# Gradient stage: silu outputs transposed by DMA as 16-bit planes, second layer moved to the end of a pair

## The reference, cut to what matters

```python
def _mlp(w1, b1, w2, b2, x):
    return jax.nn.silu(x @ w1.T + b1) @ w2.T + b2
...
k_flat = x_in.reshape(-1, D)
v_flat = out_swa.reshape(-1, D)
def loss_fn(params):
    pred = _mlp(*params, k_flat)
    return 0.5 * jnp.sum((pred - v_flat) ** 2)
grads = jax.grad(loss_fn)((w1, b1, w2, b2))
upd = jax.tree_util.tree_map(lambda p, g: (1.0 - alpha) * p - theta * g, (w1, b1, w2, b2), grads)
```

## Time and profile before

| | us |
|---|---|
| median of three runs | 2511.51 |
| profiled execution, its own time | 2516.16 |
| profiled execution, span | 2514.3 |
| gradient phase, first to last matmul in the trace | about 455 to 1458 |

### The profile page before, as it was taken

The page is one execution under the profiler, slowest core; times in us unless marked ns, Lnnn a source line. Parts: engine busy times, 40 slices in busy tenths (PEclk is TensorE's granted clock), DMA queues, the critical chain, the costliest instruction groups (busy, mean ns, idle before and its releaser), DMA issues. The chain is left out here.

```text
span 2514.3 us, 41156 instructions
## 1 busy us (share of the span) xinstructions
PE 2426.6 (97%) x15649; PEld 2158.3 (86%) x15649; DVE 1770.7 (70%) x3700; ACT 1294.1 (51%) x2270; POOL 1411.0 (56%) x940
## 2 busy tenths in 40 slices
PE   7999999799999999999999989999999879999998
PEld 6888888688888888888888877777777769999998
DVE  7777776576676776777776676667766657777766
ACT  4878788544444444444444455655665524343333
POOL 3565657566666666666666534666666544333333
PEclk9999999899999999999999999999999979999999
DMA  3222222600010010000000132232221134444441
GB/s 123 87 76 90 79 77 72 247 26 26 26 34 27 26 30 26 26 26 26 26 26 22 53 97 81 96 98 92 90 87 61 31 123 135 141 139 138 152 134 57
DMA packets 135284, 190.33 MB, mean 76 GB/s; under 512 B 13426, under 2 KB 103959, under 8 KB 134960
## 3 DMA queue, kind: packets, MB, share of 16 engines
q1 hardware_dynamic: 121264, 157.27, 19.3%
q0 software_dynamic: 13824, 30.44, 3.6%
HBM read 123.13 MB, written 72.12 MB: 78 GB/s over the span
## 5 line engine op out<-in xcount | busy, mean ns | idle before, releaser
L2178 POOL TENSOR_TENSOR m_hl<-m_hf,m_hh 128x512 fp32r<-128x512 f32 x112 | 168.8, 1519 | 146.5 <-ACT m_hh L1841 146.4
L2539 POOL DMA_INDIRECT out<-e_ys,slot_token x80 | 83.0, 1037 | 232.6 <-DVE e_ys L2495 220.1
L104 PE MATMUL e_ps_y<-r_w_h,e_hl 128*128 128x256 f32 x640 | 181.1, 283 | 0.0
L104 PE MATMUL e_ps_y<-r_w_l,e_hh 128*128 128x256 f32 x640 | 179.0, 280 | 0.0
L104 PE MATMUL e_ps_y<-r_w_h,e_hh 128*128 128x256 f32 x640 | 178.9, 280 | 0.0
L2428 ACT ACTIVATE e_hf<-e_ps_z,e_b 128x640 f32<-128x640 f32 x128 | 102.0, 797 | 147.8 <-PE e_ps_z L104 147.4
L839 POOL DMA_INDIRECT xbuf_d<-xn,scatter_rows x128 | 151.3, 1182 | 46.5 <-issue 38.1
L700 POOL TENSOR_TENSOR prob<-prob,softmax_small 128x1024 f32<-128x1024 f32 x65 | 123.1, 1894 | 71.3 <-DVE softmax_small L633 71.3
L104 PE MATMUL e_ps_z<-slotsT_h,w_l 128*128 128x320 f32 x512 | 159.4, 311 | 1.1 <-DVE slotsT_l L2473 1.1
L1190 ACT ACTIVATE dpredT_h<-dpredT 128x512 fp32r<-128x512 f32 (+1 forms) x33 | 20.6, 626 | 270.1 <-DVE dpredT L1314 264.8
L104 PE MATMUL e_ps_z<-slotsT_l,w_h 128*128 128x320 f32 x512 | 159.3, 311 | 0.0
(11 more groups left out here) (313 smaller groups left out, 9088.9 us busy)
## 6 DMA issues: line engine op xcount, KB each, us to landing
shared_x<-in_x SPq DMA_DIRECT2D x32, 512.0 KB, 4.9
shared_xT<-xT_d SPq DMA_DIRECT2D x64, 256.0 KB, 4.6
new_w1T<-in_W SPq DMA_DIRECT2D x16, 1024.0 KB
new_w2T<-in_W SPq DMA_DIRECT2D x16, 1024.0 KB, 5.8
xbuf_d<-new_w1T SPq DMA_DIRECT2D x16, 650.0 KB, 9.0
slots<-xbuf_d SPq DMA_DIRECT2D x15, 650.0 KB, 6.9
xn_d<-xn SPq DMA_DIRECT2D x32, 256.0 KB, 2.5
xT_d<-shared_xT SPq DMA_DIRECT2D x32, 256.0 KB, 2.6
```

What stands on the lines that cost most here:

```text
L104: i = e.matmul(out, a, b, start=first and not onto and n == 0, stop=last and n == len(terms) - 1, skip_group_check=onto)
L2178: e.tensor_tensor(hl[:, t, 0:N], hf[(HC * C + t) % NZ][:, 0:N], hh[:, t, 0:N], ALU.subtract).then_inc(*h_low(C, t))
L2539: e.indirect_dma_start(io["out"], bass.IndirectOffsetOnAxis(ap=token[i % 2][:, b:b + 1], axis=0), ys[:, b], None, bounds_check=NT - 1, oob ...
```

## The change

Of the 65 tiles, the 60 of pairs 2 to 31 (`by_dma`) are no longer transposed by TensorE. ScalarE copies a tile's `h_full` (128 x 1024 float32, seen as 128 x 2048 words of 16 bits) into two planes, the low words and the high words (`split_words`); one DMA of SyncE transposes both planes in 16 blocks of 128 x 128 words (`move_words`); ScalarE puts the words of each number together again (`join_words`) and rounds the result into `hTh`; GpSimd makes `hTl` (`rest_moved`). `predict` is moved to the end of the pair's round on TensorE, and waits for each half of `hTh`/`hTl` apart. Its `residual` and all that follows is moved to the start of the next round. There are four banks for `z` and four for all else. `h_h` and `h_l` have two buffers in place of four, and are made after the transposed halves. `rest_xn` and `rest_xT` come last in VectorE's round.

```diff
-ZBANKS = 3
+ZBANKS = 4
+def by_dma(g):
+    return 4 <= g < 2 * NPAIR
...
             def predict(p):
                 N, acc = blocks_of(p) * P, bank("pred", p)
-                pe.wait_ge(*hT_low.at(2 * p + blocks_of(p) - 1, 1))
                 pe.wait_ge(*freed("pred", p))
                 for m in range(KC):
                     mc = slice(m * P, (m + 1) * P)
+                    for half in range(2):
+                        ks = range(4 * half, 4 * half + 4)
+                        for b in range(blocks_of(p)):
+                            g = 2 * p + b
+                            pe.wait_ge(*(moved_low[b].at(g, half) if by_dma(g) else hT_low.at(g, half)))
...
+            for p in range(1, PAIRS):
+                g = 2 * p
+                if p >= 2:
                     forward(p, 0)
+                    transpose_d(p - 1)
+                if 2 <= p < NPAIR:
                     forward(p, 1)
+                backward(p - 1, 0)
+                backward(p - 1, 1)
+                accumulate_w2(p - 1, 0)
+                if not by_dma(g):
                     transpose_h(p, 0)
+                accumulate_w2(p - 1, 1)
+                if p < NPAIR and not by_dma(g + 1):
                     transpose_h(p, 1)
+                accumulate_w2(p - 1, 2)
+                accumulate_w2(p - 1, 3)
+                if p < NPAIR:
+                    for t in range(4):
+                        accumulate_w1(p - 1, t)
+                    predict(p)
...
+            def split_words(g):
+                b = g % 2
+                act.wait_ge(*h_half.at(g, 1))
+                act.wait_ge(*moved_low[b].at(g - 2, 1))
+                e.activation(hT_f[b][:].bitcast(U16).rearrange("p (s n) -> p s n", s=2),
+                             hf[b][:].bitcast(U16).rearrange("p (n s) -> p s n", s=2), ACTF.Copy).then_inc(*words_made[b](g))
+
+            def join_words(g):
+                b = g % 2
+                act.wait_ge(*words_moved[b].at(g))
+                e.activation(hT_f[b][:].bitcast(U16).rearrange("p (n s) -> p s n", s=2),
+                             wordsT[b][:].rearrange("p (s k) t -> p s (k t)", s=2), ACTF.Copy).then_inc(*words_joined[b](g))
+                act.wait_ge(*words_joined[b].at(g))
+                act.wait_ge(*pred_done.at(g // 2 - 1))
+                for half, hc in enumerate(cols):
+                    ks = slice(4 * half, 4 * half + 4)
+                    e.activation(hTh[:, ks, block[b]], hT_f[b][:, hc].rearrange("p (k t) -> p k t", k=4), ACTF.Copy).then_inc(*moved_high[b](g, half))
...
+            for p in range(2, PAIRS):
+                g = 2 * p
+                round_dT(p - 1)
+                forward(p, 0)
+                round_dp(p - 1)
+                if by_dma(g):
+                    split_words(g)
+                if p < NPAIR:
                     forward(p, 1)
+                    seeds(g)
+                    if by_dma(g + 1):
+                        split_words(g + 1)
+                backward(p - 1, 0)
+                if p < NPAIR:
+                    seeds(g + 1)
+                backward(p - 1, 1)
+                for b in range(blocks_of(p)):
+                    if by_dma(g + b):
+                        join_words(g + b)
...
+                for b in range(blocks_of(p)):
+                    round_h(p, b)
+                round_xn(p)
+                if p < NPAIR:
                     round_xT(p + 1)
...
+            def rest_moved(g):
+                b = g % 2
+                for half, hc in enumerate(cols):
+                    ks = slice(4 * half, 4 * half + 4)
+                    pool.wait_ge(*moved_high[b].at(g, half))
+                    e.tensor_tensor(hTl[:, ks, block[b]], hT_f[b][:, hc].rearrange("p (k t) -> p k t", k=4),
+                                    hTh[:, ks, block[b]], ALU.subtract).then_inc(*moved_low[b](g, half))
...
+            def move_words(g):
+                b = g % 2
+                sp_.wait_ge(*words_made[b].at(g))
+                sp_.wait_ge(*words_joined[b].at(g - 2))
+                e.dma_start(wordsT[b][:], hT_f[b][:].bitcast(U16), transpose=True).then_inc(*words_moved[b](g))
```

More of the change, by code:

```diff
@@ L849 @@
 TILES = 2 * NPAIR + 1
-ZBANKS = 3
+ZBANKS = 4
+def by_dma(g):
+    return 4 <= g < 2 * NPAIR
 def gradient_banks():
-    out = [("z", g, i) for g in range(4) for i in range(2)]
-    for p in range(PAIRS + 1):
-        now, both, old = p < PAIRS, p < NPAIR, p >= 1
+    z = [("z", g, i) for g in range(TILES) for i in range(2)]
+    out = [("hT", g, i) for g in range(2) for i in range(2)] + [("pred", 0), ("dT", 0)]
+    for p in range(1, PAIRS):
         g = 2 * p
[L859 to L871, removed]
+        out += [("dT", p - 1)] if p >= 2 else []
+        out += [("dh", g - 2 + b, i) for b in range(2) for i in range(2)]
+        out += [("g2", p - 1, 0)]
+        out += [("hT", g, i) for i in range(2) if not by_dma(g)]
+        out += [("g2", p - 1, 1)]
+        out += [("hT", g + 1, i) for i in range(2) if p < NPAIR and not by_dma(g + 1)]
+        out += [("g2", p - 1, t) for t in (2, 3)]
+        g1 = [("g1", p - 1, t) for t in range(4)]
+        out += g1 + [("pred", p)] if p < NPAIR else [("pred", p)] + g1[:2] + [("dT", p)] + g1[2:]
+    out += [("dh", TILES - 1, i) for i in range(2)] + [(k, NPAIR, t) for k in ("g2", "g1") for t in range(4)]
     out.append(("sums",))
-    return [u for u in out if u[0] == "z"], [u for u in out if u[0] != "z"]
+    return z, out
 def chunk_blocks(C):
@@ L978, in gradient_phase @@
         h_half, rest_made = signal("h_half", kinds["z"]), signal("rest_made", kinds["z"])
+        moved_tiles = [[g for g in tiles if by_dma(g) and g % 2 == b] for b in range(2)]
+        words_made, words_joined = ([signal(f"{n}{b}", moved_tiles[b]) for b in range(2)] for n in ("words_made", "words_joined"))
+        words_moved = [signal(f"words_moved{b}", moved_tiles[b], 16) for b in range(2)]
+        moved_high, moved_low = ([signal(f"{n}{b}", [(g, half) for g in moved_tiles[b] for half in range(2)]) for b in range(2)]
+                                 for n in ("moved_high", "moved_low"))
         hT_low, dz_half = signal("hT_low", kinds["hT"]), signal("dz_half", kinds["dh"])
@@ L1219, in scalar @@
                 seed(n)
-            forward(0, 0)
-            forward(0, 1)
+            for b in range(2):
+                forward(0, b)
+                seeds(b)
+                round_h(0, b)
             round_xT(1)
@@ L1264, in scalar @@
+            for n in range(4):
+                keep(n)
+            round_dT(NPAIR)
+            round_dp(NPAIR)
+            act.wait_ge(*chunk_in[0].at(0, final_pair(0)))
+            act.wait_ge(*pred_done.at(NPAIR))
+            e.activation(halves[0][:, 0:KC * T], shared.xT[0][:], ACTF.Copy).then_inc(*chunk_high(0))
+            final_backward()
             act.wait_ge(*z_done.at(TILES - 1, 1))
@@ L1471, in gpsimd, with slope @@
             pool = Engine(e)
-            def forward(g):
+            def slope(g):
                 t = sp[g % 4]
@@ L1529, in sync @@
                 e.dma_start(sp[2 + k][:], w2_v[:, k]).then_inc(*w2_in[k](0))
-            load_rest(0)
-            load_rest(1)
+            for p in range(2):
+                load_xn(p)
+                load_oT(p)
             xbuf_rows = [x.rearrange("(p a) d -> p (a d)", p=P) for x in io["xbuf_d"]]
```

230 lines of the change are left out of this document (118 added, 112 removed).

## The result

The changed kernel takes 2579.93 us (median of four runs, 2571.39 to 2600.14), the kernel before 2512.74 (2510.19 to 2514.90). The ratio is 1.028, with a 95% interval of 1.025 to 1.0311: slower. The forecast had the side and the range right and the size wrong: +18 us, where the medians give +67 and the two profiled executions +55.2 (2571.39 less 2516.16).

The account below looks back on a forecast made before the run. TensorE bounds the kernel before at 30.20 us a pair; after, POOL's loop of 30.5 plus 0.3 for lost turns gives 30.8. That is 0.6 more, 30 times: +18 us on 2511.5, rounded to 2530; range 2475 to 2635.

Parts of the forecast that it names:

- The walk around a pair: Gradient phase, loop through POOL, PE's `predict`, DVE and ACT: 30.5 us a pair, against 28.46 for PE's own work.
- I add 0.3 us for turns lost to POOL: DVE operations waiting through several POOL operations, three in 29 before: 0.3 us a pair, part hidden behind PE, making 30.8.
- late transfers: Rival: two serial transposing transfers exceed 12.9 us of cover; 9.0 us each gives 2683, 8.2 each 2635. Chance 0.26.
- POOL's loop: The forecast case: POOL's loop sets the pitch at 30.4 to 32.0 us a pair; chance 0.36.
- The split: ACT's copy of 2048 words into two planes per tile: 1.92 us, bounds 1.06 to 3.0; one lies on the loop.
- four `halves_l`: POOL's four new subtractions of 128x512 a pair: about 1.25 us each, 5.0 us in all.
- join: ACT's copy putting 2048 words per tile together again: 1.92 us, costed the same as the split.
- POOL's wait for `rest`: POOL's one long wait of 10.8 us a pair, to be cut into two pieces of some 3 us.
- The transfers: SyncE's two 512 KB transposing transfers a pair: costed at 4.9 us each, hidden within 12.9 us; landing in 5 to 6.
- blocks one at a time: Rival: a transfer handles its 16 blocks in turn, 20 us each, +810 us in all; chance 0.04, outside the range.
- The port: DVE operations with two SBUF inputs wait for the running POOL operation to end; by this rule alone 30.5 us a pair.
- TensorE stays the bound: Rival: `dpredT_l` gets in ahead of POOL's sum, PE's 28.46 us rules; 2475 at 29.0 a pair, best 2460. Chance 0.24.

Follow-up runs that it names:

- e5: e2 plus a second GpSimd wait, for `dpredT_l`, before the sum that opens its round: 2484.71 us, 0.9887 of the kernel before.
- e7: Changed kernel with GpSimd adding only 8 of 1024 columns into `dz_sum`, so most of the first bias's gradient is left out: 2479.43 us, ratio 0.9873.
- e2: Changed kernel with GpSimd waiting for `g_xTl` before its two `h_l`, and both tiles' sigmoids ahead of the even tile's split on ScalarE: 2491.61 us, ratio 0.9924.
- e8: Changed kernel with only the odd tile's sigmoids moved ahead of the even tile's split, no added GpSimd wait: 2582.59 us, ratio 1.0278.
- e10: Changed kernel with four small chained ScalarE copies ahead of `round_xn`, making `xn_l` ready about a microsecond later: 2583.89 us, ratio 1.0283.

## Why the prediction was wrong in its size

- **The walk around a pair, 30.5 us, was right**, for pairs that lose no turn. On its own clock (time 0 is 925.79 us, the end of the last `halves_l` before the second pair above), with `dpredT_l`, the slope and the next `halves_l` from the timeline: `dpredT_l` is asked for at 6.41 (932.20; predicted 6.3) and done at 8.54 (predicted 8.56), the first slope starts at 11.27 and the second at 15.75 (941.54; predicted 16.0), and the next pair's last `halves_l` ends at 30.29.

```profile
932.20 2.13 DVE L1391 TENSOR_TENSOR dpredT_l<-dpredT,dpredT_h 128x512 fp32r<-128x512 f32 x1 [0.70 <-ACT dpredT_h L1233]
936.28 1.91 ACT L1207 ACTIVATE hT_full<-h_full 128x2048 uint16<-128x2048 uint16 x1 [1.84 <-DVE h_full L1349]
937.06 2.42 POOL L1540 TENSOR_TENSOR silu_slope<-silu_slope,silu_rest 128x1024 f32<-128x1024 f32 x1 [3.29 <-DVE silu_rest L1354]
941.54 2.40 POOL L1540 TENSOR_TENSOR silu_slope<-silu_slope,shared_oT 128x1024 f32<-128x1024 f32 x1 [2.06 <-DVE shared_oT L1354]
951.02 5.06 POOL L1551 TENSOR_TENSOR halves_l<-hT_full,halves_h 128x512 fp32r<-128x512 f32 x4
```

- **The step that failed is "I add 0.3 us for turns lost to POOL".** It took the count of the kernel before, three in 29, and hid part of the price behind PE. The runs show 15 in 30, at 3.78 us each, 1.9 a pair. The count belonged to another operation, `g_xTl`, beside another POOL list, and there was no ground for keeping it; why half of the turns are lost here and a tenth before is not shown (before, too, three POOL operations followed without a gap where it happened). And the price was set at a time when TensorE was the bound: here the next `forward` waits for `g_xTl`, which stands behind `xn_l` on VectorE, and some or all of its first twelve matmuls then run at 1.2 GHz in 13 of the 15 pairs. With 1.9 in place of 0.3 the sum is 32.4 us a pair, against 32.05 measured.
- **That the range held is luck.** Its upper part was there for late transfers, which did not come. POOL's loop was given 32.0 us a pair at most, which is 2566 us by the prediction's own reckoning, and the median is 2580.
- **The split** took 1.91 us against 1.92 estimated; four `halves_l` took 5.06 us against 5.0. The **join** took 2.55 against 1.92; it writes in steps of two words where the split reads in them, and whether that is the reason was not tried. In the changed kernel POOL never waits for what the join makes, so it cost nothing there. TensorE was busy for 92 and 94% of the two stretches (92 predicted), ACT for 21.3 us a pair (20.6), and POOL's wait for `rest` came in two pieces, 3.3 and 2.1 us in the pair above (some 3 each).
- **The transfers** landed in 4.2, 4.3 and 6.1 us (least, median, most), against 4.9 to 6 expected. The rival of late transfers did not come to pass, nor did blocks one at a time: 16 blocks in 4.3 us. The Trainium skill, "Advanced Engine Details and Errata", section "X-Bar Transpose (TRN2)", has transposing transfers as fast as plain ones, and the trace agrees (median 4.3 us; a plain load of 512 KB from DRAM: 4.9).
- **The port.** The Trainium skill, "SBUF — State Buffer", section "Who interferes with whom", has an exclusive lock under which the second engine blocks. The runs agree as far as blocking goes. They do not agree with what the prediction read into it, that the second one comes in when the running instruction has finished: in 15 of 30 pairs it did not until POOL ran out of work. So read, the rule gave 30.5 us a pair; the measured mean is 32.05.
- **TensorE stays the bound**, the rival on the faster side, failed for the reason given against it: `dpredT_l` came into POOL's sum in each pair that lost no turn (2.08 to 2.33 us). It becomes nearly true when the loop is cut: e5 29.18, e7 29.12.

## What to carry to other kernels

When work is moved to GpSimd next to VectorE operations with two SBUF inputs, look for a run of GpSimd operations without a gap, and for which VectorE operation falls ahead of it: it may wait for one operation or for all of them. One GpSimd wait on VectorE's result (1.2 us of GpSimd's time a pair here, 0.35 us of the pitch) makes the order certain; here it was worth 53 us. A rare event in a trace is not a small term: ask what its count and price hang on, and price it anew where the bound moves. And test a shorter loop together with what holds it back, since e2's edit was worth 35 us in one setting and nothing in the other.

## What the runs showed that was not expected

- A VectorE operation of 0.69 us took 7.1 to 8.5 us, waiting through up to four GpSimd operations on end, in 15, 17 and 19 of 30 pairs of three kernels (changed, e8, e10), most of them in every second pair; asking a microsecond later did not help. In the same kernels `g_xTl`, asked for directly behind an `xn_l` that got its turn, took 2.9 us and never more.
- After an idle time of 3.5 to 3.7 us TensorE ran its next twelve matmuls at 1.2 GHz in five pairs (0.43 us apart), at 2.4 GHz in two (0.23 us apart), and fell from the one to the other on the way in eight. A lost turn costs 4.4 to 4.7, 2.2 and 3.4 to 3.8 us in these. The length of the idle time does not tell them apart: it was 3.74 us in one of the five and 3.73 us in the two.
- A copy of 2048 words of 16 bits on ScalarE takes 1.91 us reading in steps of two words, and 2.55 us writing in them.
